# Attention values divided once per tile, loads issued in parts, row sums on ScalarE for both output matrices, six banks for turned weights, and new instruction lists

## Chip, cores and metric

The kernel runs on one core of one Trainium2 chip. The metric is the device time of one execution in microseconds; three runs were timed, and their median counts. One further execution was recorded by the profiler.

## What is computed

The input is x of shape 2 x 4096 x 512 in f32. Two residual blocks follow each other, each behind a layer norm over the 512 channels. Cut to what matters:

```python
# block 1 (RWKV mixing): xn = layernorm(x)
k = xn @ Wk.T ; r = xn @ Wr.T ; v = r
y = wkv_scan(-exp(time_decay), time_first, k, v)   # recurrence over the 4096 positions of each batch
x = x + (sigmoid(r) * y) @ Wo.T
# block 2: xn = layernorm(x); h = rmsnorm(xn, gamma1)
q = h @ Wq + bq ; kv = (h @ Wdown + bdown) @ Wup + bup      # 16 heads of 32, latent 64
att = softmax(q[t, h] . k[t, g] / sqrt(32), over g)         # heads of ONE position attend to each other
xb = xn + (att @ v) @ Wo + bo
h2 = rmsnorm(xb, gamma2) ; gate = softmax(h2 @ Wg + bg)     # 8 experts, all of them computed
x = x + xb + sum_e gate[e] * (h2 @ We[e])
```

Products of f32 numbers are made from f16 pairs: every operand is split into a high and a low half, and three matmuls (high-high, low-high, high-low) stand for one.

## The kernel before

**Tiles.** The 8192 positions are cut into 32 tiles of 256 positions, with the two batches in turn. A tile passes through three stages: mixing (steps `pre_*`, `mix_*`), attention over heads (`att_*`) and the closing stage (`fin_*`, `moe_gate`, `moe`). The last holds 16 units `moe 0` to `moe 15` (8 experts by 2 halves of the tile), each 12 matmuls into one of two PSUM banks, from which VectorE adds the gated result to `acc` (L1311). Unit u + 2 on TensorE waits until unit u has been added.

**Order.** Each engine works through a list written out in the file: `PE_HEAD`, `PE_ORDER`, `PE_TAIL`, and the same for `DVE` (VectorE), `ACT` (ScalarE), `POOL` (GpSimd) and `SP` (SyncE, which issues the DMAs). An entry is (step, part, tile). `pipeline` runs the head once, the order 27 times (once for each tile in the middle) and the tail once. Several tiles are in work at a time: an iteration of the loop finishes units of one tile while it runs the attention of the next and the mixing of the one after. Waits stand inside the steps. A step that waits holds back all that stands behind it in its engine's list.

**Set-up.** The head of each list also prepares the weights. `set_load` and `set_experts` on SyncE load all of them; the weights lie in homes borrowed from tiles that are used later. `set_max` on VectorE takes the largest absolute value of every row block, `set_bound` on GpSimd the largest over the partitions, `set_scale` on VectorE the scales made from it. For the experts the bound is a row sum of absolute values instead, made on ScalarE (`set_abs`, L782). The matrices `k`, `r` and `o1` are turned by TensorE (`set_turn`, L1346) into `turned(n)`, which is one of two PSUM banks in turn; ScalarE writes the high half (`set_hi`, L772) and VectorE the low half (`set_lo`, L1090). The experts are scaled in place (`set_times`, L788), split by ScalarE (L770), and their low half is made on GpSimd (L686).

**Attention's end.** For k = 0 to 7, `att_probs k` on TensorE makes 4 groups of 66 columns in one bank: 32 values' high parts and the sum of the probabilities, then 32 low parts and a column of zeros. `att_probs k` on VectorE divides by the sum: a reciprocal of 4 columns (L1250), a reduction that adds high and low part (L1251) and a product (L1253). `fin_back` then transposes `on` in 32 x 32 blocks (L1261), ScalarE writes the high half (L911), VectorE the low half, and `fin_project` on TensorE uses them. The bank of `att_probs k` on TensorE is free for `k + 2` when L1251 has read it.

In ScalarE's head list, all 16 steps `set_abs` of the experts stand ahead of `mix_turn` of tile 0:

```python
    ("set_decay", 0, -1), ("pre_norm", 0, 0), ("set_k", 0, -1), ("set_k", 1, -1), ("set_r", 0, -1),
    ("set_abs", 0, -1), ("set_abs", 1, -1), ("set_abs", 2, -1), ("set_r", 1, -1), ("set_abs", 3, -1),
    ...
    ("set_abs", 13, -1), ("set_o1", 1, -1), ("set_abs", 14, -1), ("set_abs", 15, -1), ("mix_turn", 0, 0),
```

Of the kernel before, what the change touches and what calls it, by code (L numbers as in the profile page):

```python
# [122 lines left out]
def att_before(use):  # L123
# [45 lines left out]
    ("att_scores", 7, 4), ("att_probs", 6, 4), ("moe", 8, 5), ("att_probs", 7, 4), ("mix_turn", 0, 2), ("moe", 9, 5),  # L169
    ("mix_k", 0, 2), ("mix_v", 0, 2), ("att_turn", 0, 3), ("fin_project", 0, 4), ("att_latent", 0, 3),  # L170
    ("att_q", 0, 3), ("moe", 10, 5), ("att_up", 0, 3), ("moe", 11, 5), ("moe", 12, 5), ("moe", 13, 5), ("moe", 14, 5),
    ("moe", 15, 5), ("att_max", 0, 3), ("fin_turn2", 0, 4), ("att_max", 1, 3), ("fin_gate", 0, 4), ("moe", 0, 4),
    ("moe", 1, 4), ("att_max", 2, 3), ("att_max", 3, 3), ("moe", 2, 4), ("att_m", 0, 3), ("moe", 3, 4), ("moe", 4, 4),
    ("att_scores", 0, 3), ("att_scores", 1, 3), ("moe", 5, 4), ("att_probs", 0, 3), ("att_scores", 2, 3),
    ("moe", 6, 4), ("att_probs", 1, 3), ("att_scores", 3, 3), ("att_probs", 2, 3), ("att_scores", 4, 3),
    ("moe", 7, 4), ("att_probs", 3, 3), ("att_scores", 5, 3), ("moe", 8, 4), ("att_probs", 4, 3),
    ("att_scores", 6, 3), ("att_probs", 5, 3), ("att_scores", 7, 3), ("mix_project", 0, 2), ("att_probs", 6, 3),
    ("att_probs", 7, 3), ("mix_turn", 0, 1), ("moe", 9, 4), ("mix_k", 0, 1), ("mix_v", 0, 1), ("att_turn", 0, 2),
    ("moe", 10, 4), ("moe", 11, 4), ("att_latent", 0, 2), ("att_q", 0, 2), ("moe", 12, 4), ("att_up", 0, 2),
    ("moe", 13, 4), ("moe", 14, 4), ("fin_project", 0, 3), ("moe", 15, 4), ("att_max", 0, 2), ("att_max", 1, 2),  # L180
    ("fin_turn2", 0, 3), ("att_max", 2, 2), ("att_max", 3, 2), ("att_m", 0, 2), ("att_scores", 0, 2),
    ("att_scores", 1, 2), ("moe", 0, 3), ("att_probs", 0, 2), ("att_scores", 2, 2), ("att_probs", 1, 2),
    ("att_scores", 3, 2), ("fin_gate", 0, 3), ("moe", 1, 3), ("att_probs", 2, 2), ("att_scores", 4, 2),
    ("att_probs", 3, 2), ("att_scores", 5, 2), ("mix_project", 0, 1), ("att_probs", 4, 2), ("att_scores", 6, 2),
    ("moe", 2, 3), ("att_probs", 5, 2), ("att_scores", 7, 2), ("att_probs", 6, 2), ("moe", 3, 3), ("moe", 4, 3),
    ("att_probs", 7, 2), ("moe", 5, 3), ("moe", 6, 3), ("moe", 7, 3), ("moe", 8, 3), ("att_turn", 0, 1),
# [1405 lines left out]
```

## Time and profile before

| | |
|---|---|
| median of 3 runs | 2910.02 us (2909.48 to 2913.99) |
| the profiled execution | 2906.95 us, its span 2905.1 us |
| TensorE (PE) busy, share of the span | 2618.6 us, 90% |
| VectorE (DVE) | 2453.4 us, 84% |
| ScalarE (ACT) | 1522.6 us, 52% |
| GpSimd (POOL) | 1006.4 us, 35% |
| mean granted TensorE clock | 0.978 |
| chain that ended last, by engine | PE 54%, DVE 32%, ACT 6% |

The span runs from the first to the last instruction. Busy time counts the work that an engine did, not its waits. In rows with an "idle before" the arrow names what ended the wait. A timeline row that says x24 stands for 24 instructions merged.

### The profile page before, as it was taken

To read this page: it belongs to the slowest core of one execution; us is meant where nothing else is said; L and a number is where in the kernel's file an instruction comes from. 1 tells how busy PE (TensorE), PEld (TensorE's weight loads), DVE (VectorE), ACT (ScalarE), POOL (GpSimd) and SP (SyncE) were. 2 spreads that over 40 slices of the span, in tenths; PEclk is the share of its full clock that TensorE was granted. 3 is DMA by queue.
4 is the path that set the end of the run, shared out by engine and by line. 5 is a ranking of instruction groups with operands and counts; after the bars stand their busy time and mean duration, and the time that the engine had idled before them with its cause. 6 is when DMAs were issued, how large, how long until landed. Compare 5 with 4: busy or idle time off the path is not lost.

```text
span 2905.1 us, 49052 instructions
## 1 busy us (share of the span) xinstructions
PE 2618.6 (90%) x18896; PEld 1579.7 (54%) x18896; DVE 2453.4 (84%) x4353; ACT 1522.6 (52%) x2783; POOL 1006.4 (35%) x970
## 2 busy tenths in 40 slices
PE   2447999999999999999999999999999999999899
PEld 2324555555556555555655555555555555565454
DVE  5688888889888888988888898888889888888853
ACT  5664555555555555555555555555555555554531
POOL 0354333334333333433333343333333333333320
PEclk9768999999999999999999999999999999999999
DMA  6011111111111101111110111111011111111110
GB/s 213 15 30 30 38 37 16 29 32 37 38 37 32 21 26 35 37 38 38 23 30 23 38 37 37 37 23 28 26 37 38 38 38 22 26 28 37 30 23 15
DMA packets 579083, 102.51 MB, mean 35 GB/s; under 512 B 547346, under 2 KB 547474, under 8 KB 578834
## 3 DMA queue, kind: packets, MB, share of 16 engines
q1 hardware_dynamic: 578852, 99.39, 16.5%
q8 instruction: 150, 2.46, 0.4%
q14 instruction: 81, 0.66, 0.1%
HBM read 48.49 MB, written 16.78 MB: 22 GB/s over the span
## 4 chain that ended last, share of the span: by engine, by line
PE 54%; DVE 32%; ACT 6%; issue 4%; POOL 2%; SPq 1%; DMA 0%; DVEq 0%; ACTq 0%; POOLq 0%
PE bank L1333 49%; DVE wkv L1134 4%; DVE ks L1219 3%; PE bank L1355 3%; DVE acc L1311 3%; DVE zz L1158 2%; DVE wkv L1123 2%; DVE e L1147 2%; DVE ev L1167 2%; DVE on L1253 2%; DVE zz L1130 2%; DVE mcol L1234 1%; DVE h2t L1096 1%; ACT ot L923 1%; DVE hrow L1225 1%
## 5 line engine op out<-in xcount | busy, mean ns | idle before, releaser
L1333 PE MATMUL bank<-w_e,h2t 128*128 128x512 f16 x6144 | 1392.8, 380 | 72.9 <-DVE acc L1311 52.6
L1333 PEld LDWEIGHTS bank<-w_e,h2t 128*128 128x128 f16 x6144 | 587.3, 98 | 754.6 <-DVE acc L1311 77.1
L1311 DVE SCALAR_TENSOR_TENSOR acc<-bank,gates,acc 128x512 f32<-128x512 f32 x512 | 376.6, 741 | 136.6 <-PE bank L1333 132.3
L727 POOL TENSOR_TENSOR pr<-pr 128x512 f16<-128x512 f32 x256 | 307.1, 1200 | 281.9 <-ACT pr L901 279.2
L899 ACT ACTIVATE pr<-bank,plog,col 128x512 f32<-128x512 f32 x256 | 197.1, 770 | 201.0 <-PE bank L1501 201.0
L1134 DVE TENSOR_TENSOR_SCAN wkv<-e,wkv 128x256 f32<-128x256 f32 x256 | 255.9, 1040 | 22.9 <-ACT e L827 19.6
L696 POOL TENSOR_TENSOR zz<-wkv,zz 128x512 f32<-128x512 f32 x64 | 106.7, 1667 | 432.2 <-DVE ev L1145 432.2
L1333 PE MATMUL bank<-w_o,xo 128*128 128x512 f16 x768 | 176.1, 387 | 49.7 <-DVE xo L1096 49.5
L1158 DVE RECIPROCAL zz<-zz 128x256 f32<-128x256 f32 x128 | 218.5, 1729 | 0.0
L901 ACT ACTIVATE pr<-bank,plog,col 128x512 f16<-128x512 f32 x256 | 197.0, 770 | 0.0
L1333 PE MATMUL bank<-xo,w_k 128*128 128x256 f16 x1536 | 175.6, 275 | 12.0 <-DVE xo L1096 12.0
L1234 DVE TENSOR_REDUCE mcol<-bank 128x4 f32<-128x512 f32 x256 | 160.7, 681 | 19.0 <-PE bank L1488 19.0
L1333 PE MATMUL bank<-w_o,oo 128*128 128x512 f16 x768 | 172.6, 382 | 0.9 <-DVE oo L1096 0.9
L1333 PE MATMUL bank<-xo,w_r 128*128 128x256 f16 x1536 | 172.9, 273 | 0.0
L1333 PE MATMUL bank<-ht,w_q 128*128 128x256 f16 x1536 | 172.9, 273 | 0.0
L1333 PEld LDWEIGHTS bank<-xo,w_k 128*128 128x128 f16 x1536 | 149.2, 99 | 31.6 <-DVE xo L1096 12.9
L1333 PEld LDWEIGHTS bank<-ht,w_q 128*128 128x128 f16 x1536 | 150.3, 98 | 17.4
L1333 PEld LDWEIGHTS bank<-xo,w_r 128*128 128x128 f16 x1536 | 150.2, 98 | 17.4
L1333 PEld LDWEIGHTS bank<-w_o,xo 128*128 128x128 f16 x768 | 73.7, 99 | 141.9 <-DVE xo L1096 55.2
L709 POOL TENSOR_TENSOR x<-x,bo_row 128x512 f32<-128x512 f32 x64 | 92.5, 1466 | 161.8 <-ACT x L854 161.8
L743 POOL TENSOR_TENSOR acc<-x,x 128x512 f32<-128x512 f32 x64 | 80.3, 1276 | 173.1 <-DMA result<-acc 173.1
L714 POOL TENSOR_TENSOR qo<-t,qo 128x256 f16<-128x256 f32 x128 | 109.4, 862 | 84.6 <-ACT qo L884 84.6
(197 smaller groups left out, 4297.7 us busy)
## 6 DMA issues: line engine op xcount, KB each, us to landing
qs<-qo SPq DMA_DIRECT2D x384, 64.0 KB, 2.4
xk<-in_attn_x SPq DMA_DIRECT2D x32, 512.0 KB, 4.8
x<-in_attn_x SPq DMA_DIRECT2D x32, 512.0 KB, 3.9
result<-acc SPq DMA_DIRECT2D x32, 512.0 KB, 2.8
ks<-k SPq DMA_DIRECT2D x128, 64.0 KB, 2.4
w_e<-in_ffn_We SPq DMA_DIRECT2D x7, 1024.0 KB, 14.2
qs<-in_attn_Wk SPq DMA_DIRECT2D x1, 1024.0 KB, 5.8
ks<-in_attn_Wr SPq DMA_DIRECT2D x1, 1024.0 KB, 8.0
```

The lines of the kernel that those rows point to most:

```text
L696: nc.gpsimd.tensor_tensor(zz[:, :, :], wkv[:, 2, :, 0:T], zz[:, :, :], ALU.add).then_inc(mix_pool.sem, 1)
L709: nc.gpsimd.tensor_tensor(x2[:, s, :], x2[:, s, :], bo_row[:, :], ALU.add).then_inc(att_pool.sem, 1)
L714: nc.gpsimd.tensor_tensor(grouped(dst, 1)[:, :, b, :], t32[:, b % 2, :].rearrange("p (g j) -> p g j", g=G), grouped(dst, 0)[:, :, b, :], A ...
L727: nc.gpsimd.tensor_tensor(pr16[:, 1, k % 2, :], pr[:, k % 2, :], pr16[:, 0, k % 2, :], ALU.subtract).then_inc(att_pool.sem, 1)
L899: nc.scalar.activation(pr[:, k % 2, :], att_bank[ATT_BANK["S", k]][:, :], ACT.Exp, bias=plog[:, 0:1], scale=colof["soft"])\
L901: nc.scalar.activation(pr16[:, 0, k % 2, :], att_bank[ATT_BANK["S", k]][:, :], ACT.Exp, bias=plog[:, 0:1], scale=colof["soft"])\
L1134: V.tensor_tensor_scan(wkv[:, n, c, 1:T + 1], e1[:, c, :], src[:, c, :], wkv[:, n, c, 0:1], ALU.mult, ALU.add).then_inc(mix_dve.sem, 1)
L1158: V.reciprocal(zz[:, c, :], zz[:, c, :]).then_inc(mix_dve.sem, 1)
L1219: V.tensor_copy(ks[n * HD:(n + 1) * HD, :, f, :], grouped(k16, 0)[f * HD:(f + 1) * HD].rearrange("p g b j -> p g (b j)")).then_inc(att_dve ...
L1234: V.tensor_reduce(mcol[:, 4 * k:4 * k + 4], att_bank[ATT_BANK["M", k]][:, :].rearrange("p (g x) -> p g x", g=4), AX, ALU.max).then_inc(att ...
L1311: V.scalar_tensor_tensor(out=acc[:, s, :], in0=moe_bank[u % 2][:, :], scalar=gates[:, s, e:e + 1], in1=acc[:, s, :], op0=ALU.mult, op1=ALU ...
L1333: ins = nc.tensor.matmul(dst, left(a), right(b), start=(n == 0), stop=(n == last))
```

## The change

1. `att_probs` on VectorE keeps only the reduction, which now covers 33 columns (32 values and the sum) and writes into `on`, widened from 32 to 33 columns a group. `fin_back` begins with one reciprocal of 32 sums and one product over the whole 128 x 1024 tile, each waited for, before the transpose.
2. `set_load` is cut into five parts and `set_experts` into eight, in the same order as before. The residual rows of tile 0 (`mix_k 0`) are now loaded ahead of the masks.
3. `o1` and `o2` are bounded by ScalarE's row sums too (8 more blocks in `set_abs`, `SUMMED`), no longer by `set_max` on VectorE.
4. `turned(n)` goes through six PSUM banks.
5. All lists are new. In ScalarE's head `mix_turn` of tile 0 now stands third, and `set_abs` is spread between the steps of tile 0; `mix_k` and `mix_v` of tile 0 stand ahead of `set_o1` on TensorE; the scaling and splitting of the experts stands later.

```diff
-MAXED = ["k", "r", "o1", "q", "o2", "small", "experts"]
+MAXED = ["k", "r", "q", "small", "experts"]
+SUMMED = ["o1", "o2"] + [f"e{e}" for e in range(E)]
+TURN_BANKS = [0, 1, 4, 5, 6, 7]
...
-        on = sb("on", [P, G, HD])
+        on = sb("on", [P, G, HD + 1])
...
-            return bank[n % 2][:, :]
+            return bank[TURN_BANKS[n % len(TURN_BANKS)]][:, :]
...
-                name = f"e{k // 2}"
+                name = SUMMED[k // 2]
...
             def att_probs(t, k):
                 pv = att_bank[ATT_BANK["PV", k]][:, 0:4 * VW].rearrange("p (g d) -> p g d", g=4)
-                og = on[:, 4 * k:4 * k + 4, :]
...
-                V.reciprocal(rden[:, 4 * k:4 * k + 4], pv[:, :, HD]).then_inc(att_dve.sem, 1)
-                V.tensor_reduce(og, pv.rearrange("p g (l d) -> p g d l", l=2)[:, :, 0:HD, :], AX, ALU.add).then_inc(att_dve.sem, 1)
-                dve.wait_ge(*att_dve.done(t, "norm", 3 * k + 1))
-                V.tensor_tensor(og, og, rden[:, 4 * k:4 * k + 4].unsqueeze(2).to_broadcast([P, 4, HD]), ALU.mult).then_inc(att_dve.sem, 1)
+                V.tensor_reduce(on[:, 4 * k:4 * k + 4, :], pv.rearrange("p g (l d) -> p g d l", l=2), AX, ALU.add).then_inc(att_dve.sem, 1)
...
-                    dve.wait_ge(summed, E * CB)
-                V.transpose(ot32.rearrange("p b (g j) -> p g b j", g=G), on[:, :, :].rearrange("p g (b j) -> p g b j", b=CB)).then_inc(fin_dve.sem, 1)
+                    dve.wait_ge(summed, len(SUMMED) * CB)
+                V.reciprocal(rden[:, :], on[:, :, HD]).then_inc(fin_dve.sem, 1)
+                dve.wait_ge(*fin_dve.done(t, "den"))
+                V.tensor_tensor(on[:, :, 0:HD], on[:, :, 0:HD], rden[:, :].unsqueeze(2).to_broadcast([P, G, HD]), ALU.mult).then_inc(fin_dve.sem, 1)
+                dve.wait_ge(*fin_dve.done(t, "quot"))
+                V.transpose(ot32.rearrange("p b (g j) -> p g b j", g=G), on[:, :, 0:HD].rearrange("p g (b j) -> p g b j", b=CB)).then_inc(fin_dve.sem, 1)
...
-                    if n >= 2:
-                        pe.wait_ge(lo_done, n - 1)
+                    if n >= len(TURN_BANKS):
+                        pe.wait_ge(lo_done, n - len(TURN_BANKS) + 1)
```

The loop's lists, cut to where the order differs (both begin at another point of the same circle):

```diff
 PE_ORDER, from unit 2 on
-    ("moe", 2, 3), ("moe", 3, 3), ("att_scores", 0, 2), ("att_scores", 1, 2), ("moe", 4, 3), ("moe", 5, 3), ("att_probs", 0, 2),
-    ("att_scores", 2, 2), ("att_probs", 1, 2), ("att_scores", 3, 2), ("moe", 6, 3), ("att_probs", 2, 2),
-    ("att_scores", 4, 2), ("moe", 7, 3), ("att_probs", 3, 2), ("att_scores", 5, 2), ("att_probs", 4, 2),
-    ("att_scores", 6, 2), ("mix_project", 0, 1), ("att_probs", 5, 2),
-    ("att_scores", 7, 3), ("mix_turn", 0, 1), ("moe", 8, 4), ("att_probs", 6, 3), ("att_probs", 7, 3), ("mix_k", 0, 1),
+    ("moe", 2, 3), ("moe", 3, 3), ("att_scores", 0, 2), ("moe", 4, 3), ("att_scores", 1, 2), ("moe", 5, 3), ("att_probs", 0, 2),
+    ("att_scores", 2, 2), ("att_probs", 1, 2), ("att_scores", 3, 2), ("moe", 6, 3), ("att_probs", 2, 2),
+    ("att_scores", 4, 2), ("att_probs", 3, 2), ("att_scores", 5, 2), ("moe", 7, 3), ("att_probs", 4, 2),
+    ("att_scores", 6, 3), ("att_probs", 5, 3), ("att_scores", 7, 3), ("mix_project", 0, 2), ("att_probs", 6, 3),
+    ("att_probs", 7, 3), ("mix_turn", 0, 1), ("moe", 8, 4), ("mix_k", 0, 1),
 DVE_ORDER, from unit 0 on
-    ("moe", 0, 3), ("moe", 1, 3), ("att_m", 0, 2), ("mix_sum", 1, 1), ("moe", 2, 3), ("mix_value", 1, 2), ("mix_scan", 1, 2),
-    ("moe", 3, 4), ("mix_rec", 2, 2), ("moe", 4, 4), ("moe", 5, 4), ("att_probs", 0, 3), ("att_probs", 1, 3),
-    ("mix_rec", 3, 2), ("mix_gate", 1, 2), ("att_probs", 2, 3), ("mix_split", 1, 2), ("pre_stats", 0, 1),
+    ("moe", 0, 4), ("moe", 1, 4), ("att_m", 0, 3), ("mix_sum", 1, 2), ("mix_value", 1, 2), ("moe", 2, 4), ("moe", 3, 4),
+    ("mix_scan", 1, 2), ("mix_rec", 2, 2), ("moe", 4, 4), ("moe", 5, 4), ("mix_rec", 3, 2), ("att_probs", 0, 3),
+    ("att_probs", 1, 3), ("mix_gate", 1, 2), ("att_probs", 2, 3), ("att_probs", 3, 3), ("mix_split", 1, 2),
...
-    ("moe", 8, 4), ("att_probs", 6, 3), ("att_probs", 7, 3), ("att_stats", 0, 2), ("att_norm", 0, 2), ("fin_back", 0, 3),
-    ("mix_decay", 0, 1), ("att_turn", 0, 2), ("moe", 9, 4), ("mix_sum", 0, 1), ("mix_value", 0, 1),
+    ("att_probs", 6, 3), ("att_probs", 7, 3), ("att_stats", 0, 2), ("att_norm", 0, 2), ("fin_back", 0, 3),
+    ("mix_decay", 0, 1), ("moe", 8, 4), ("att_turn", 0, 2), ("moe", 9, 4), ("mix_sum", 0, 1), ("mix_value", 0, 1),
```

In GpSimd's loop `mix_sum 1` now stands ahead of `att_rest` instead of behind it, and in ScalarE's loop `mix_num 1` stands behind `att_scores 3` instead of behind `att_scores 0`.

## Rows read from the trace of the kernel before

**Rows 1.** Busy time per engine in stretches; x counts instructions.

```profile
core 0: us, PE busy (x) PEld busy (x) DVE busy (x) ACT busy (x) POOL busy (x), PEclk, DMA share, GB/s
0.00:62.00 62.00, 13.35 (x56) 11.12 (x56) 30.77 (x97) 31.16 (x82) 2.07 (x11) 1.00 0.77 250
...
126.00:253.00 127.00, 67.59 (x531) 49.60 (x529) 101.33 (x150) 84.11 (x156) 67.51 (x64) 0.74 0.17 26
...
400.00:2600.00 2200.00, 2090.84 (x15247) 1260.30 (x15246) 1948.55 (x3423) 1171.19 (x2120) 789.03 (x753) 1.00 0.16 32
2592.00:2906.00 314.00, 290.62 (x1949) 163.49 (x1947) 205.10 (x379) 124.79 (x227) 82.82 (x83) 0.97 0.13 24
...
1486.59:1571.65 85.06, 80.80 (x596) 48.79 (x593) 75.46 (x133) 45.22 (x82) 30.29 (x29) 1.00 0.17 32
```

**Rows 2.** TensorE's waits, 400 to 2600 us: total us, times, longest.

```profile
PE bank L1333 <- DVE acc L1311: 50.1, 51, 2.0
PE bank L1512 <- DVE on L1251: 19.8, 24, 0.8
PE bank L1333 <- DVE h2t L1096: 19.5, 26, 1.0
PE bank L1333 <- DVE xo L1096: 12.5, 24, 0.5
```

**Rows 3.** Groups of VectorE's instructions over the whole span.

```profile
L1311 DVE SCALAR_TENSOR_TENSOR acc<-bank,gates,acc 128x512 f32<-128x512 f32 x512 | 376.6, 741 | 136.6 <-PE bank L1333 132.3 <-issue 0.7
L1134 DVE TENSOR_TENSOR_SCAN wkv<-e,wkv 128x256 f32<-128x256 f32 x256 | 255.9, 1040 | 22.9 <-ACT e L827 19.6
L1158 DVE RECIPROCAL zz<-zz 128x256 f32<-128x256 f32 x128 | 218.5, 1729 | 0.0
...
L1253 DVE TENSOR_TENSOR on<-on,rden 128x128 f32<-128x128 f32 x256 | 130.5, 510 | 8.8
...
L1251 DVE TENSOR_REDUCE on<-bank 128x128 f32<-128x256 f32 x256 | 100.3, 392 | 0.0
...
L1250 DVE RECIPROCAL rden<-bank 128x4 f32<-128x4 f32 x256 | 43.4, 170 | 12.2 <-PE bank L1513 12.2
...
L1229 DVE TENSOR_TENSOR vp<-hrow,vp 128x1024 f16<-128x1024 f32 x32 | 39.0, 1219 | 1.1 <-ACT vp L906 1.1
```

**Rows 4.** Instructions on tile `on`: shortest, median, longest in ns.

```profile
L1253 DVE TENSOR_TENSOR on<-on,rden x256: 291/292/1296, 185.4 to 2842.2; 128x128 f32<-128x128 f32 x128
```

**Rows 5.** Timeline of TensorE, where tile 3's and tile 17's `mix_k` begin.

```profile
295.60 2.67 PE L1333 MATMUL bank<-xo,w_k 128*128 128x256 f16 x23
...
1486.59 5.40 PE L1333 MATMUL bank<-xo,w_k 128*128 128x256 f16 x48
```

**Rows 6.** Timeline of TensorE, the two largest waits of one iteration.

```profile
1464.98 2.76 PE L1333 MATMUL bank<-w_e,h2t 128*128 128x512 f16 x12 [1.60 <-DVE acc L1311]
...
1475.54 0.20 PE L1512 MATMUL bank<-vp,pr 128*128 128x66 f16 x1 [0.83 <-DVE on L1251]
```

**Rows 7.** Timeline of VectorE in that iteration.

```profile
1459.13 1.75 DVE L1147 TENSOR_TENSOR e<-e,v 128x512 f32<-128x512 f32 x1
...
1494.67 1.29 DVE L1096 SCALAR_TENSOR_TENSOR oo<-ot,oo 128x512 f16<-128x512 f32 x2 [1.79 <-ACT oo L911]
```

**Rows 8.** Timeline of ScalarE at the start.

```profile
37.39 0.63 ACT L782 ACTIVATE ot<-w_e 128x512 f32<-128x512 f32 x1 [10.63 <-DMA w_e<-in_ffn_We]
...
60.50 0.63 ACT L782 ACTIVATE ot<-acc 128x512 f32<-128x512 f32 x1
...
79.00 0.69 ACT L813 ACTIVATE v<-bank,col 128x512 f32<-128x512 f32 x1 [1.93 <-PE bank L1333]
...
82.94 6.22 ACT L788 ACTIVATE w_e<-w_e,scl 128x512 f32<-128x512 f32 x10
```

**Rows 9.** Timeline of TensorE at the start.

```profile
66.68 7.04 PE L1333 MATMUL bank<-xo,w_k 128*128 128x256 f16 x48 [10.43 <-DVE xo L1096]
...
112.50 7.98 PE L1333 MATMUL bank<-w_o,xo 128*128 128x512 f16 x24 [33.53 <-DVE xo L1096]
```

More of the change, by code:

```diff
@@ L166 @@
+    ("att_scores", 5, 2), ("moe", 7, 3), ("att_probs", 4, 2),
 ]
 PE_TAIL = [
[L169 to L186, printed above, removed]
-    ("moe", 9, 3), ("moe", 10, 3), ("moe", 11, 3), ("att_latent", 0, 1), ("att_q", 0, 1), ("moe", 12, 3),
@@ L217 @@
-    ("pre_norm", 0, 2), ("set_g", 0, -1), ("mix_project", 0, 1), ("mix_turn", 0, 2), ("att_probs", 2, 0),
-    ("att_probs", 3, 0), ("att_probs", 4, 0), ("att_probs", 5, 0), ("mix_decay", 0, 2), ("att_probs", 6, 0),
-    ("att_probs", 7, 0), ("att_stats", 0, 1), ("att_norm", 0, 1), ("fin_back", 0, 0), ("mix_sum", 0, 2),
-    ("att_turn", 0, 1), ("mix_value", 0, 2), ("mix_scan", 0, 2), ("fin_project", 0, 0), ("att_latent", 0, 1),
-    ("mix_rec", 0, 2), ("mix_rec", 1, 2), ("mix_gate", 0, 2), ("mix_split", 0, 2), ("mix_decay", 1, 2),
@@ L222 @@
[L222 to L224 removed]
+    ("mix_turn", 0, 0), ("set_scale", 0, -1), ("set_max", 2, -1), ("set_k", 0, -1), ("set_k", 1, -1),
+    ("set_r", 0, -1), ("set_r", 1, -1), ("set_max", 3, -1), ("mix_decay", 0, 0), ("set_scale", 1, -1),
+    ("mix_sum", 0, 0), ("mix_value", 0, 0), ("mix_scan", 0, 0), ("mix_rec", 0, 0), ("mix_rec", 1, 0),
@@ new lines @@
+    ("mix_gate", 0, 0), ("set_o1", 0, -1), ("mix_split", 0, 0), ("mix_decay", 1, 0), ("set_o1", 1, -1),
+    ("mix_sum", 1, 0), ("mix_value", 1, 0), ("mix_scan", 1, 0), ("mix_rec", 2, 0), ("mix_rec", 3, 0),
+    ("mix_gate", 1, 0), ("mix_split", 1, 0), ("pre_stats", 0, 1), ("pre_norm", 0, 1), ("set_max", 4, -1),
+    ("set_q", 0, -1), ("set_q", 1, -1), ("mix_project", 0, 0), ("mix_turn", 0, 1), ("set_d", 0, -1),
+    ("att_stats", 0, 0), ("set_scale", 2, -1), ("att_norm", 0, 0), ("mix_decay", 0, 1), ("set_u", 0, -1),
@@ new lines @@
+    ("pre_stats", 0, 2), ("mix_split", 1, 1), ("att_probs", 0, 0), ("att_probs", 1, 0), ("pre_norm", 0, 2),
+    ("mix_project", 0, 1), ("mix_turn", 0, 2), ("set_g", 0, -1), ("att_probs", 2, 0), ("att_probs", 3, 0),
+    ("mix_decay", 0, 2), ("att_probs", 4, 0), ("att_probs", 5, 0), ("att_probs", 6, 0), ("att_probs", 7, 0),
+    ("att_stats", 0, 1), ("att_norm", 0, 1), ("mix_sum", 0, 2), ("mix_value", 0, 2), ("mix_scan", 0, 2),
+    ("att_turn", 0, 1), ("mix_rec", 0, 2), ("att_latent", 0, 1), ("fin_back", 0, 0), ("mix_rec", 1, 2),
@@ L243 @@
-    ("mix_gate", 1, 3), ("att_probs", 0, 4), ("moe", 5, 5), ("mix_split", 1, 3), ("att_probs", 1, 4),
-    ("att_probs", 2, 4), ("moe", 6, 5), ("pre_stats", 0, 2), ("att_probs", 3, 4), ("att_probs", 4, 4),
-    ("pre_norm", 0, 2), ("moe", 7, 5), ("att_probs", 5, 4), ("mix_project", 0, 3), ("att_probs", 6, 4),
-    ("att_probs", 7, 4), ("mix_turn", 0, 2), ("fin_back", 0, 4), ("att_stats", 0, 3), ("att_norm", 0, 3),
-    ("moe", 8, 5), ("mix_decay", 0, 2), ("att_turn", 0, 3), ("mix_sum", 0, 2), ("mix_value", 0, 2),
@@ new lines @@
+    ("att_probs", 4, 4), ("moe", 6, 5), ("mix_project", 0, 3), ("att_probs", 5, 4), ("mix_turn", 0, 2),
+    ("att_probs", 6, 4), ("moe", 7, 5), ("att_probs", 7, 4), ("att_stats", 0, 3), ("fin_back", 0, 4),
+    ("att_norm", 0, 3), ("moe", 8, 5), ("mix_decay", 0, 2), ("att_turn", 0, 3), ("mix_sum", 0, 2),
+    ("mix_value", 0, 2), ("fin_project", 0, 4), ("mix_scan", 0, 2), ("moe", 9, 5), ("mix_rec", 0, 2),
+    ("att_latent", 0, 3), ("mix_rec", 1, 2), ("mix_gate", 0, 2), ("moe", 10, 5), ("moe", 11, 5), ("mix_split", 0, 2),
@@ new lines @@
+    ("att_probs", 2, 3), ("att_probs", 3, 3), ("mix_split", 1, 2), ("pre_stats", 0, 1), ("att_probs", 4, 3),
+    ("pre_norm", 0, 1), ("moe", 6, 4), ("moe", 7, 4), ("mix_project", 0, 2), ("mix_turn", 0, 1), ("att_probs", 5, 3),
+    ("att_probs", 6, 3), ("att_probs", 7, 3), ("att_stats", 0, 2), ("moe", 8, 4), ("att_norm", 0, 2),
+    ("mix_decay", 0, 1), ("fin_back", 0, 3), ("att_turn", 0, 2), ("moe", 9, 4), ("moe", 10, 4), ("mix_sum", 0, 1),
+    ("mix_value", 0, 1), ("fin_project", 0, 3), ("mix_scan", 0, 1), ("mix_rec", 0, 1), ("mix_rec", 1, 1),
@@ L388 @@
+    ("att_m", 0, 1), ("moe_store", 0, 2), ("moe_store", 0, 1),
 ]
```

403 lines of the change are left out of this document (207 added, 196 removed), and 3 rows, old and new, of the table POOL_HEAD.

## The prediction

> **What bounds the kernel now.** I read first the busy time by stretches, then TensorE's waits, then the timelines of one iteration and of the start.
>
> In the middle of the run TensorE is busy 2090.84 of 2200 us at full granted clock, VectorE 1948.55, and nothing else is near [rows 1]. So the loop is bound by TensorE, and its idle time is what a better VectorE or a better order can give. From tile 3's `mix_k` to tile 17's, 14 iterations take 1486.59 - 295.60 = 1190.99 us, 85.07 each [rows 5]; in one of them TensorE works 80.80 us and stands 4.26 [rows 1]. Nearly all of that is VectorE being late: per iteration (26 of them in the window) 1.93 us for an eviction of an expert unit, 0.76 for the reduction behind `att_probs`, 0.75 for `h2t`, 0.48 for `xo` [rows 2]. It is the same in every iteration: the two largest waits stand in the timeline as 1.60 and 0.83 us [rows 6]. The most that 27 iterations can give is 27 x 4.26 = 115 us.
>
> The head is another kernel. Over the first 62 us ScalarE is busy 31.16 us and TensorE 13.35 [rows 1]: ScalarE waits 10.63 us for the first expert's weights, sums until 60.50 + 0.63 us, and only then turns to tile 0 [rows 8]; TensorE starts `mix_k` at 66.68 and `mix_project` at 112.50, after 33.53 us for VectorE [rows 9]. The steady order begins with tile 3 at 295.60 [rows 5].
>
> **The change part by part.**
>
> *One division per tile.* Eight times a tile VectorE loses a reciprocal of 170 ns and a product of 510 ns [rows 3]. The product alone takes 291 ns (shortest and median); the mean is 510 because the slowest take 1296 [rows 4]. These stood beside a GpSimd instruction on f32 tiles, as did the 1.75 us instruction at 1459.13 [rows 7]. Removed: 8 x (0.170 + 0.510) = 5.4 us busy. Added: eight columns more in each reduction, under 0.1 us in all by 392 ns for 256; a reciprocal of 32 columns, between 0.17 us (4) and 1.73 us (256) [rows 3], taken by a straight line as 0.36; a product of 1024 elements, bounded by 1.22 us for 1024 elements with two SBUF sources below [rows 3] and by eight times 0.51 = 4.1 above; I take 1.22, because a single instruction meets GpSimd once and in that iteration GpSimd has no work there. Net 5.4 - 0.1 - 0.36 - 1.22 = 3.7 us of 75.46 on VectorE.
>
> Where it lies: the 1.6 us added stand in `fin_back`, ahead of the low half `oo`, which waits 1.79 us for ScalarE today [rows 7]. ScalarE is late there because it evicts `mix_k` and normalises first, so the added work is covered; without that cover it would push back `mix_decay`, `moe 8` and `att_turn` by 1.6. The rows of 33 columns are read by the transpose with another stride; no row shows that, I take nothing, and if it cost the transpose half again (0.6 us) VectorE's saving would still be 3.1.
>
> What the saving and the new order are worth I work out by walking one iteration through both lists, with a unit of 12 matmuls at 2.6 us start to start, an eviction at 0.74, a scan at 1.04 [rows 3] and the other steps at their lengths in that iteration's timeline. In the profile, units 2 and 3 end at 1460.2, but `mix_value` (one instruction held to 1.75 us [rows 7] by GpSimd's `att_rest`) and `mix_scan` keep VectorE from evicting unit 3 until 1464.9, and unit 5 starts at 1464.98 [rows 6]. In the new lists `att_rest` stands behind `mix_sum`, `mix_value` ends at about 1458.7, units 2 and 3 are evicted by 1461.2, and TensorE runs units 4 and 5 without a wait, to 1466.3 instead of 1467.6. VectorE then has `mix_scan`, `mix_rec 2`, units 4 and 5 and `mix_rec 3` until 1469.0. `att_probs 0` to `2` on TensorE are not held; `att_probs 3`, which now follows `att_scores 4` at once, waits about 0.7 us for GpSimd's low half (1470.9). `mix_split` on VectorE ends at about 1474.5, `mix_project` starts at 1475.0 instead of 1476.67, the next `mix_k` at 1484.9 instead of 1486.59 [rows 5]. From there to unit 2 the neighbours are the old ones, with their 0.75 for `h2t`. So 1.7 us, of which the waits give 1.60 + 0.83 + 0.48 = 2.9 and the new one takes 0.7, the rest being small new delays. The second half of the walk gives some tenths more; I take 1.8 us an iteration. Bounds: 0 (each wait removed comes back elsewhere, VectorE still being 84% busy) and 3.2 (three quarters of the 4.26 go). 27 x 1.8 = 49 us, with 0 to 86.
>
> *What is moved past.* The eviction of unit 8 stood ahead of `att_probs 6` and now stands behind `fin_back` and `mix_decay`. TensorE's unit 10 waits for it. By the walk it ends 1.2 us before TensorE asks.
>
> The Trainium skill, GPSIMD Engine Reference, Key points, says that GpSimd shares its SBUF interfaces with VectorE and contends with VectorE instructions that have two SBUF inputs. The spread from 291 to 1296 ns agrees [rows 4]. By that rule the new long product could be held for one GpSimd instruction, about 1 us by that spread, and the saving would be 2.7 instead of 3.7 us.
>
> *The head.* ScalarE's `mix_turn` no longer waits for the experts' sums. TensorE's `mix_k` of tile 0 then needs only the low half of `k`: the six banks and the order put that at about 23 us instead of 66.68. But ScalarE still has the sums of the first expert ahead of its eviction of `k`, and the weights arrive at 37.39 as before, since the loads keep their order. So that eviction comes at about 39, that of `v` at 42 instead of 79.00 [rows 8]: 37 us earlier. From there to `mix_project` it took 112.50 - 79.00 = 33.5 us. In the new lists `set_scale 1` and `set_o1` (by their instructions' count and lengths in the timeline an estimated 4.5 and 2.8 us) and on ScalarE 14 steps of two sums stand between, and the experts' low halves on GpSimd, which slowed the last products by 1.6 us, are gone. Walked through, `mix_scan` of the first half begins at about 48, its `mix_split` ends at 61, the second half at 79: `mix_project` about 33 us earlier. Loads cut into parts cost nothing: same DMAs, same order. The 4.6 us of `set_max` for `o1` and `o2` go, but VectorE waited for the constants there anyway.
>
> Then some is given back. Behind that point the new lists have on ScalarE all 32 blocks of `set_times` (0.61 us each by 6.22 for ten [rows 8]) and the splits, of which some 18 us were done earlier, and on VectorE an estimated 8 us of `set_d`, `set_u`, `set_o2` and `set_scale 2`, less the 3.7 us of the division. From 126 to 253 us VectorE was busy 101.33 of 127 and ScalarE 84.11 [rows 1]; both have room for this, but not without friction. I take 3 us lost: head 30 us. Bounds: 38 (nothing given back, and the shorter divisions used) and 12 (the 18 us of ScalarE all on the path, and 3 more).
>
> *The tail.* 314 us with 290.62 of TensorE [rows 1]; two more tiles pass attention and closing stage there. 2 x 1.8, so 4 us, with 0 to 8.
>
> **Sum.** Against the profiled execution of 2906.95 us: -30 - 49 - 4 = 2824. The median is 3.07 above that execution, so 2827 us.
>
> **The rivals.**
>
> *The loop gives nothing (B).* TensorE's waits move to other places. For it: VectorE is 89% busy in the loop, and the order around `h2t` is unchanged. Against it: the two largest waits have a named cause that the new order removes. 2910 - 30 - 3 = 2877.
>
> *The loop closes nearly up (C).* The 0.7 us at `att_probs 3` does not come, and what VectorE saves pulls all evictions forward. 2910 - 30 - 86 - 3 = 2791.
>
> *The head's gain is given back (E).* Tile 0's `fin_turn2` waits on ScalarE for all experts' low halves. GpSimd starts them some 14 us of work later in its list. If that ends last, and the loop gives nothing, the time stays within 6 us of 2910. Against it: GpSimd was busy 67.51 of 127 us there [rows 1].
>
> *Slower (D): unit 8's eviction.* If `fin_back` is not covered (1.6 us), is held by GpSimd (1.0) and then misses ScalarE again (1.8), the eviction comes 4.4 us later, 3.2 us past the margin of 1.2, in each iteration. Then 27 x (3.2 - 1.8) = 38 us are lost, the head's 30 gained: 2918. It decides from 4.1 us of delay on. Against it: the eviction of `mix_k` by ScalarE, not `fin_back`, sets the time of `oo` today. That the lengthened product is the start of this delay is what the rule of the GPSIMD page would give.
>
> **How the numbers follow.** A 0.60, B 0.17, C 0.15, E 0.03, D 0.05. The predicted time is A's, 2827, its own range 2795 to 2862 (loop 1 to 2.9 us an iteration, head 20 to 35). The range for 8 in 10 takes in B and most of C: 2783 to 2882. A change of 0.2% is about what a measurement of this kernel can tell from none. Faster by more than that: A, B, C, 0.92. Within it: E, 0.03. Slower: D, 0.05.
>
> **What would show it.** In the profile after: TensorE's `mix_k` of tile 0 starts near 23 us and `mix_project` near 79; the iteration is 83.3 us, with no wait over 1 us for an eviction of units 4 or 5; L1251's group is alone in `att_probs` at about 0.40 us, and one product of about 1.2 us a tile stands in `fin_back`; tile 3's `mix_k` starts near 266 us. The prediction is wrong if `att_probs` or unit 10 on TensorE collects a new wait of over 2 us, if the long product takes 3 us or more, or if tile 0's `fin_turn2` waits for the experts' low halves.

## The result, and the profile after

The changed kernel takes 2795.18 us (2793.62 to 2796.41, 4 runs) against 2910.86 us before on the same chip: a ratio of 0.9601, 95% interval 0.9584 to 0.9617. It is 4% faster. That is 32 us less than predicted, inside the range, and at the value of rival C (2791) rather than of the case I had held likeliest, at the very edge of whose own range (2795 to 2862) it lies.

Busy time per engine in stretches after, to be read against [rows 1]; the fourth line is the last 313 us, most of the tail:

```profile
core 0: us, PE busy (x) PEld busy (x) DVE busy (x) ACT busy (x) POOL busy (x), PEclk, DMA share, GB/s
0.00:62.00 62.00, 22.84 (x152) 19.17 (x152) 34.52 (x99) 29.87 (x71) 4.79 (x13) 0.80 0.82 257
126.00:253.00 127.00, 78.63 (x581) 50.80 (x582) 102.19 (x155) 95.65 (x171) 80.87 (x73) 0.75 0.17 32
400.00:2500.00 2100.00, 2057.07 (x15115) 1254.51 (x15114) 1797.16 (x3021) 1165.31 (x2096) 727.88 (x742) 1.00 0.17 33
...
2480.00:2794.00 314.00, 293.74 (x1933) 163.02 (x1930) 197.72 (x332) 124.07 (x226) 81.55 (x83) 0.97 0.13 25
```

In the middle of the run TensorE is now busy 98% of the time (95% before) and VectorE 86% (89%). In the one iteration whose two windows stand further down VectorE works 44.64 + 25.63 = 70.3 us, where 75.46 stood [rows 1]: 5.2 us less. TensorE's waits in that stretch, total us, times, longest:

```profile
PE bank L1343 <- DVE h2t L1106: 18.5, 25, 0.7
PE bank L1522 <- POOL pr L736: 15.6, 27, 0.7
PE bank L1343 <- DVE acc L1321: 8.8, 25, 0.6
```

Of the four waits of [rows 2], the one for `on` and the one for `xo` have left the list, the one for `acc` is down from 50.1 to 8.8 us, `h2t` is as it was, and one has come: for GpSimd's low half of `pr`. Together they are 42.9 us in 25.6 iterations, 1.7 us an iteration; before, TensorE stood 4.26 us in one.

TensorE's timeline: start and length of `mix_k` and `mix_v` of tile 0 and of `mix_project` of tile 0, of tile 3's `mix_k`, and in the middle of the run one iteration's start, its wait for `h2t`, and its end:

```profile
24.41 6.40 PE L1343 MATMUL bank<-xo,w_k 128*128 128x256 f16 x48
42.96 7.34 PE L1343 MATMUL bank<-xo,w_r 128*128 128x256 f16 x48 [12.15 <-ACT xk L816]
85.61 8.17 PE L1343 MATMUL bank<-w_o,xo 128*128 128x512 f16 x24 [33.56 <-DVE xo L1106]
...
263.86 5.40 PE L1343 MATMUL bank<-xo,w_k 128*128 128x256 f16 x48
...
1411.12 5.40 PE L1343 MATMUL bank<-xo,w_k 128*128 128x256 f16 x48
...
1457.20 2.76 PE L1343 MATMUL bank<-w_e,h2t 128*128 128x512 f16 x12 [0.74 <-DVE h2t L1106]
...
1493.05 5.40 PE L1343 MATMUL bank<-xo,w_k 128*128 128x256 f16 x48
```

These starts give the account used for every run below: how early the steady order begins (tile 3's `mix_k`), what an iteration takes (tile 3's `mix_k` to tile 30's, divided by 27), and the tail (from there to the end of the span). Head, loop and tail of the changed kernel: 263.86, 81.95 and 316.5 us; of the kernel before 295.60, 85.04 and 313.5 us. The gain of 112.1 us in the span is so 31.7 from the head, 83.4 from the loop (27 x 3.09), and -3.0 from the tail. The prediction had 30, 49 and 4. (The medians are 115.7 us apart, since the profiled execution of the kernel before was 3.9 us faster than its median.)

The division, by the instructions on tile `on` (shortest, median, longest in ns) that answer to [rows 3, 4]:

```profile
L1259 DVE TENSOR_REDUCE on<-bank x256: 369/423/433, 154.2 to 2725.6; 128x132 f32<-128x264 f32 x128
L1267 DVE RECIPROCAL rden<-on x32: 344/348/353, 194.7 to 2728.8; 128x32 f32<-128x32 f32 x32
L1269 DVE TENSOR_TENSOR on<-on,rden x32: 1224/1225/1682, 195.1 to 2729.1; 128x1024 f32<-128x1024 f32 x32
L1271 DVE STREAM_TRANSPOSE ot<-on x32: 1245/1245/1246, 196.8 to 2730.4; 128x1024 f32<-128x1024 f32 x32
```

### The profile page after: what moved, and what is told of

Same layout as the page of the kernel before. It is cut to its first block, busy times and chain, and to the rows that moved or that the text cites. A ratio compares the mean times of both kernels' runs of the same rounds, so it can differ in the third digit from the quotient of the medians.

```text
span 2793.0 us, 48627 instructions
## 1 busy us (share of the span) xinstructions
PE 2605.8 (93%) x18896; PEld 1583.4 (57%) x18896; DVE 2292.0 (82%) x3903; ACT 1532.3 (55%) x2799; POOL 950.7 (34%) x970
## 4 chain that ended last, share of the span: by engine, by line
PE 81%; DVE 8%; ACT 5%; POOL 2%; issue 2%; SPq 1%; DVEq 0%; ACTq 0%; POOLq 0%
PE bank L1343 72%; PE bank L1365 3%; DVE mcol L1244 2%; PE bank L1481 2%; PE bank L1511 2%; DVE h2t L1106 1%; ACT pr L910 1%; POOL pr L736 1%; PE bank L1522 1%; DVE acc L1321 1%; ACT pr L908 1%; POOL w_e L695 1%; PE bank L1498 1%; ACT h2t L941 1%; DVE ks L1229 1%
## 5 line engine op out<-in xcount | busy, mean ns | idle before, releaser
L1144 DVE TENSOR_TENSOR_SCAN wkv<-e,wkv 128x256 f32<-128x256 f32 x256 | 245.0, 997 | 17.9 <-ACT e L836 16.7
L816 ACT ACTIVATE xk<-bank,col 128x512 f32<-128x512 f32 x64 | 43.8, 687 | 195.4 <-PE bank L1343 195.4
L723 POOL TENSOR_TENSOR k<-t,k 128x256 f16<-128x256 f32 x128 | 94.4, 738 | 141.4 <-ACT k L893 138.1
```

Of the source, the lines that this page charges most:

```text
L723: nc.gpsimd.tensor_tensor(grouped(dst, 1)[:, :, b, :], t32[:, b % 2, :].rearrange("p (g j) -> p g j", g=G), grouped(dst, 0)[:, :, b, :], A ...
L1144: V.tensor_tensor_scan(wkv[:, n, c, 1:T + 1], e1[:, c, :], src[:, c, :], wkv[:, n, c, 0:1], ALU.mult, ALU.add).then_inc(mix_dve.sem, 1)
```

## The experiments

Two ideas stood against each other from here. Theory O: the time comes from the orders of work (the new lists). Theory V: it comes from the work that VectorE no longer has (one division per tile). All runs in one table; head, loop and tail as above, from one profiled execution each, and each ratio against the kernel before on the same chip:

| kernel | mix_k of tile 0 | of tile 3 | iteration | tail | median us | ratio to before (95%) |
|---|---|---|---|---|---|---|
| before | 66.68 | 295.60 | 85.04 | 313.5 | 2910.86 | |
| changed | 24.41 | 263.86 | 81.95 | 316.5 | 2795.18 | 0.9601 (0.9584 to 0.9617) |
| e1_bank_division | 23.75 | 265.67 | 84.71 | 319.5 | 2872.57 | 0.9867 (0.9852 to 0.9882) |
| e2_division_alone | 69.08 | 295.67 | 83.21 | 316.3 | 2859.89 | 0.982 (0.9805 to 0.9834) |
| e3_sums_first | 61.49 | 285.23 | 81.97 | 315.8 | 2818.56 | 0.9679 (0.9663 to 0.9695) |
| e4_two_banks | 29.50 | 269.98 | 81.97 | 316.0 | 2801.32 | 0.9621 (0.9607 to 0.9635) |
| e5_first_tile_ahead | 23.31 | 253.35 | 81.98 | 318.3 | 2788.22 | 0.9573 (0.9556 to 0.959) |
| e6_unit7_ahead | 23.60 | 263.35 | 85.16 | 319.1 | 2883.70 | 0.9903 (0.9888 to 0.9917) |
| e8_scan_ahead | 22.67 | 263.55 | 82.82 | 316.4 | 2820.03 | 0.9686 (0.9671 to 0.97) |
| e9_product_twice | 22.63 | 263.82 | 82.00 | 318.9 | 2798.49 | 0.961 (0.9596 to 0.9625) |
| e10_unit3_early | 69.27 | 295.01 | 82.62 | 315.1 | 2843.24 | 0.9773 (0.9759 to 0.9786) |
| e11_unit3_unit7 | 71.61 | 297.83 | 82.70 | 318.4 | 2843.66 | 0.9774 (0.976 to 0.9787) |
| e12_tail_unit | 22.98 | 251.29 | 81.99 | 319.9 | 2786.96 | 0.9575 (0.9562 to 0.9588) |

Two cautions for the table. Kernels with the same head differ at tile 3 by up to 2.8 us (295.01 to 297.83; 263.35 to 265.67; 253.35 and 251.29), so a difference of that size in the head is not a reading. And tile 30's `mix_k` stands in the tail's list of TensorE, which in the old lists has one expert unit more ahead of it (unit 9): 70 units are left from there on, 71 in the new lists. So with the old lists 2.6 us of work counts in the loop, 0.10 us an iteration, that with the new lists counts in the tail.

**Lists without the division, division without the lists.** e1 is the changed kernel with the old steps of `att_probs` and `fin_back`:

```diff
-                V.tensor_reduce(on[:, 4 * k:4 * k + 4, :], pv..., AX, ALU.add)
+                V.reciprocal(rden[:, 4 * k:4 * k + 4], pv[:, :, HD])
+                V.tensor_reduce(og, pv...[:, :, 0:HD, :], AX, ALU.add)
+                V.tensor_tensor(og, og, rden[...].to_broadcast([P, 4, HD]), ALU.mult)
```

> The changed kernel with its new lists, but with the division made for each bank again (reciprocal, reduction and product eight times a tile, nothing added in fin_back). Theory O (the new order gives the loop its gain): the iteration stays at 82.0 to 82.8 us and the time at 2795 to 2820. Theory V (the VectorE time set free gives it): VectorE has 4 to 5 us more in each iteration, TensorE waits for evictions again, the iteration is 84.3 us or more and the time 2860 or more.

e2 is the reverse edit in the kernel before: the division once per tile, all lists, heads and banks as they were.

> The kernel before with its old lists, and only the division moved to fin_back, once per tile. Theory O: the wait of 1.6 us for the eviction of unit 3 stays, as mix_scan still stands ahead of it; only the 0.8 at att_probs shrinks: iteration 84.2 to 85.1 us, time 2885 to 2912. Theory V: the iteration falls under 83.3 us and the time under 2860.

Both went against theory O. The iteration, old lists first: 85.04 with the old division and 83.21 with the new; in the new lists 84.71 and 81.95. So the division gives 1.83 us in the old lists and 2.76 in the new; the lists give 0.33 with the old division and 1.26 with the new. Nothing adds up singly: 1.83 + 0.33 is 2.16, and both together give 3.09. The median distance from one `mix_k` to the next between tiles 3 and 29, which leaves out the unit named above, says the same: 84.97 and 83.07 us in the old lists, 84.73 and 81.92 in the new, so 1.90 and 0.24 singly and 3.05 together. The waits say why. First e1, 400 to 2500 us; then one iteration of e2 (its wait for unit 5, as in [rows 6]):

```profile
PE bank L1522 <- DVE on L1261: 34.9, 50, 1.0
PE bank L1365 <- ACT xk L802: 27.6, 25, 1.1
PE bank L1343 <- DVE h2t L1106: 17.8, 24, 0.7
PE bank L1343 <- DVE xo L1106: 9.2, 25, 0.4
PE bank L1343 <- DVE acc L1321: 8.9, 25, 0.9
```

```profile
1522.70 2.76 PE L1333 MATMUL bank<-w_e,h2t 128*128 128x512 f16 x12 [1.60 <-DVE acc L1311]
```

In e1 the new order has removed the 1.60 us for unit 3's eviction, but with eight divisions among the same steps VectorE is late at the next places: TensorE waits twice for `on` (0.98 and 0.41 us), 0.37 us for `xo`, and then, at its `mix_turn`, 1.10 us for ScalarE's `pre_norm`, which has itself stood 4.13 us for VectorE's `nb`. In e2 the division has removed the waits for `on` and `xo`, and the 1.60 us, which is a matter of order alone, is untouched. The head belongs to the rest of the change (lists, loads, sums and banks), not to the division: tile 3's `mix_k` stands at 265.67 in e1, at 295.67 in e2.

**Which order.** e8 puts, in the changed kernel, VectorE's evictions of units 2 and 3 where they were around `mix_value` and `mix_scan`:

```diff
-("mix_value", 1, 2), ("moe", 2, 4), ("moe", 3, 4), ("mix_scan", 1, 2),
+("moe", 2, 4), ("mix_value", 1, 2), ("mix_scan", 1, 2), ("moe", 3, 4),
```

> The changed kernel with VectorE's evictions of units 2 and 3 around mix_value and mix_scan again, as in the old list. If this order is what the new list adds to the division: TensorE waits 1.5 us or more for the eviction of unit 3, iteration 83.0 to 83.6, time 2822 to 2840. Rival (with VectorE's spare time the order no longer matters): under 82.3, time under 2805.

It cost 0.87 us an iteration (82.82), somewhat less than expected. Its waits:

```profile
PE bank L1523 <- POOL pr L737: 24.9, 27, 1.0
PE bank L1344 <- DVE acc L1322: 24.6, 50, 0.6
```

Unit 5 waits only 0.63 us, not 1.60: `mix_value` is not held by GpSimd in this kernel (its second product takes 0.69 us in the mean, not 1.75), which had been the other half of that delay. Beside it the wait for `pr` is longer, 0.96 us for 0.58. e10 does the opposite from the other side: the kernel before, with the new division and one move, unit 3's eviction ahead of `mix_scan`:

```diff
-("mix_value", 1, 2), ("mix_scan", 1, 2), ("moe", 3, 4),
+("mix_value", 1, 2), ("moe", 3, 4), ("mix_scan", 1, 2),
```

> The old lists and heads, the new division, and one move in VectorE's list of the loop: unit 3's eviction stands ahead of mix_scan 1 instead of behind it. Single-move theory: what the lists bring to the loop once the division is out of it (83.21 us to 81.95 us per iteration) comes mostly from this order, since its reverse cost the changed kernel 0.87 us: iteration 82.2 to 82.5 us, median 2832 to 2840 us. Joint theory: the lists bring it only together (the removed wait for unit 3 returns at the next wait, for GpSimd's low half or for unit 7's bank): iteration 82.9 to 83.2 us, median 2851 to 2860 us. The head is the old one in both: tile 3's mix_k at 295 to 296 us.

It fell between the two (82.62): the wait of 1.60 us is gone, and 1.02 of it has come back three steps later, at `att_probs 1`, as this line of its timeline shows:

```profile
1515.71 0.19 PE L1513 MATMUL bank<-vp,pr 128*128 128x66 f16 x1 [1.02 <-POOL pr L728]
```

So one transposition of two entries holds 0.59 of the 1.26 us that the lists are worth beside the new division. TensorE, no longer held at unit 5, arrives at `att_probs 1` before GpSimd has the low half; in the changed kernel the wait for GpSimd stands at `att_probs 3` and is 0.58. What holds the other 0.67 us was not taken apart.

**Unit 7.** e6 is the changed kernel with unit 7 at its old place in TensorE's list, e11 is e10 with unit 7 at its new one:

```diff
-("att_scores", 4, 2), ("att_probs", 3, 2), ("att_scores", 5, 2), ("moe", 7, 3),
+("att_scores", 4, 2), ("moe", 7, 3), ("att_probs", 3, 2), ("att_scores", 5, 2),
```

> The changed kernel with unit 7 on TensorE ahead of att_probs 3 again, the old place. If the 0.6 us for GpSimd's low half is simply covered: iteration 81.3 to 81.5, time 2779 to 2786. Rival (att_scores 5 comes later by a unit, and ScalarE's mix_split behind it too, so mix_project waits for xo): iteration 81.9 to 82.6, time 2793 to 2815.

> As the run before, and in TensorE's list unit 7 stands behind att_scores 5 instead of behind att_scores 4. Single-move theory for unit 7: its reverse cost the changed kernel 3.2 us, so the two moves together should reach 81.9 to 82.2 us per iteration and 2824 to 2831 us. Rival: the place of unit 7 matters only where GpSimd, ScalarE and mix_project stand as in the new lists; with the old ones, in which mix_project comes ahead of att_probs 5 and gives it cover, the move gives nothing or costs up to 0.6 us (a wait for GpSimd's low half at att_probs 3 as in the changed kernel): the iteration is that of the run before, or up to 0.6 us longer.

e6 was the surprise of the study, outside both of its expectations: 3.2 us more an iteration, 88 us in all, for one unit moved by two entries to fill a wait of 0.6 us. Its largest wait, then what stands around it in one iteration, and the windows over the wait and over the `mix_project` behind it (PEclk is 1.00 in the rest of the iteration):

```profile
PE bank L1523 <- POOL pr L737: 60.1, 25, 2.4
```

```profile
1444.90 0.19 PE L1523 MATMUL bank<-vp,pr 128*128 128x66 f16 x1 [2.41 <-POOL pr L737]
...
1445.36 7.04 PE L1344 MATMUL bank<-w_o,xo 128*128 128x512 f16 x24
```

```profile
1442.00:1445.30 3.30, 0.89 (x25) 0.75 (x22) 1.41 (x3) 3.22 (x5) 1.15 (x1) 1.00 0.00 0
1445.30:1452.40 7.10, 7.10 (x34) 2.99 (x32) 5.21 (x12) 3.14 (x5) 3.14 (x4) 0.76 0.00 0
```

The unit had been the cover of ScalarE's and GpSimd's chain for the scores 5, and without it `att_probs 5` stands 2.41 us. Then comes a second bill: `mix_project` takes 7.04 us where it takes 5.35 elsewhere, at a mean granted clock of 0.76, so part of it ran at the lower level (1.2 GHz). 2.41 us of new wait and 1.69 us of slower matmuls, less the 0.58 us of the wait that went, make 3.5, against 3.2 measured; the slower `mix_project` comes in 25 of the 27 iterations and the wait in 26, which makes it 3.3. In the 3.30 us of the first window TensorE had been busy 0.89, with matmuls of 0.19 and 0.38 us. The Trainium skill, TensorE: Matmul & The Clock Gate, What's actually happening, says that the granted clock is set by how busy TensorE has been recently; the trace agrees in that the clock fell behind this nearly idle stretch. The length of the wait does not settle it: the first such wait of e6 was as long, and `mix_project` behind it took 5.35 us at a clock of 1.00.

```profile
337.58 0.19 PE L1523 MATMUL bank<-vp,pr 128*128 128x66 f16 x1 [2.42 <-POOL pr L737]
338.04 5.35 PE L1344 MATMUL bank<-w_o,xo 128*128 128x512 f16 x24
```

In the old lists, where another order of the neighbours stands around it, the move of unit 7 does nothing: e11 has e10's iteration, waits and median, as the rival said.

**The long product.** e9 does the product in `fin_back` twice, which adds 1.2 us ahead of `oo`:

```diff
+                V.tensor_tensor(ot..., on[:, :, 0:HD], rden[...].to_broadcast([P, G, HD]), ALU.mult)
                 V.tensor_tensor(on[:, :, 0:HD], on[:, :, 0:HD], rden[...].to_broadcast([P, G, HD]), ALU.mult)
```

> The changed kernel with a second product of 1.22 us in fin_back, whose result is overwritten. If fin_back is covered by the 2.55 us that oo waits for ScalarE: no change, 2792 to 2799. Rival (it pushes back mix_decay, unit 8 and att_turn, each iteration by 1.2): 2815 or more.

The iteration is 82.00 instead of 81.95 us, the median 2798.49 us, both as expected if it is covered: the cover behind which I put the product is there, and has room for a second. In the changed kernel VectorE's timeline shows it, 2.55 us of waiting for ScalarE behind the product and the transpose:

```profile
1414.16 1.23 DVE L1269 TENSOR_TENSOR on<-on,rden 128x1024 f32<-128x1024 f32 x1
...
1419.21 1.29 DVE L1106 SCALAR_TENSOR_TENSOR oo<-ot,oo 128x512 f16<-128x512 f32 x2 [2.55 <-ACT oo L920]
```

**The head.** e3 lets ScalarE bound all the experts' weights before tile 0 again (all 20 entries of `set_abs` stand ahead of `mix_turn`, four for `o1` and `o2` among them, and VectorE's half of `mix_turn` comes later). e4 takes four of the six banks away; with two, ScalarE's `mix_num` must also stand ahead of `set_o1 1`, since else ScalarE, TensorE and VectorE wait for each other in a ring:

```diff
-TURN_BANKS = [0, 1, 4, 5, 6, 7]
+TURN_BANKS = [0, 1]
```

> The changed kernel with all row sums on ScalarE ahead of mix_turn of tile 0 again, as before, and VectorE's mix_turn of tile 0 moved behind set_max 3 so that nothing deadlocks. Theory O (tile 0 waited for the sums): mix_project of tile 0 at about 105 to 115 us, tile 3's mix_k 20 to 30 us later than 263.9, time 2815 to 2828. Rival (the head's gain is the work taken off VectorE and the six banks): under 8 us later, time under 2804.

> The changed kernel with two banks for turned weights instead of six, and ScalarE's mix_num 0 of tile 0 ahead of the second half of set_o1, without which the order would deadlock. If the banks save no time themselves: mix_k of tile 0 up to 5 us later, but ScalarE evicts k only at 42 us anyway, so the time stays within 2791 to 2799. Rival (the banks carry part of the head's gain): 2800 or more.

e3, as its theory O had it: tile 3's `mix_k` 21.4 us later, the loop untouched. e4, as its rival had it: `mix_k` of tile 0 5.1 us later, tile 3's 6.1, 6 us in the median. So of the 31.7 us some 21 are the sums' new place and some 6 the banks (with the one entry moved beside them), if the two simply add; the remainder was not taken apart.

e5 mends the new order where the profile after showed it waiting. `mix_k` was done at 31, but TensorE's `mix_v` stood 12.15 us for ScalarE's eviction of `k`, which stood behind the first expert's sums. ScalarE stands 10.43 us ahead of them, as its timeline in the changed kernel shows (the row names no releaser; in [rows 8] it is the transfer of these weights):

```profile
40.91 0.63 ACT L791 ACTIVATE ot<-w_e 128x512 f32<-128x512 f32 x1 [10.43 <-issue]
...
42.15 1.24 ACT L816 ACTIVATE xk<-bank,col 128x512 f32<-128x512 f32 x2
...
50.34 0.69 ACT L822 ACTIVATE v<-bank,col 128x512 f32<-128x512 f32 x1 [1.93 <-PE bank L1343]
```

```diff
-("set_abs", 3, -1), ("set_abs", 4, -1), ("mix_k", 0, 0), ("set_abs", 5, -1), ("mix_v", 0, 0), ("mix_exp", 0, 0),
+("set_abs", 3, -1), ("mix_k", 0, 0), ("mix_v", 0, 0), ("mix_exp", 0, 0), ("set_abs", 4, -1), ("set_abs", 5, -1),
```

with `mix_decay 0` ahead of `set_max 3` in VectorE's head.

> The changed kernel, with ScalarE's evictions of k and v of tile 0 and its first exponentials ahead of the sums of the first expert (which must wait for that expert's weights until 40.9 us), and VectorE's mix_decay 0 ahead of the wait for the constants. If that wait is what ends last in the head: v evicted at about 39 us instead of 50.3, mix_project of tile 0 at 74 to 80 instead of 85.6, tile 3's mix_k 5 to 11 us earlier than 263.9, time 2784 to 2790. Rival (GpSimd's low halves of the experts, 10% of the chain of waits from 60 to 264 us, end last): under 2 us earlier, 2793 to 2797.

TensorE's timeline of e5: `mix_v` follows `mix_k` at once, and `mix_project` starts 10.5 us earlier.

```profile
23.31 6.25 PE L1345 MATMUL bank<-xo,w_k 128*128 128x256 f16 x48
29.70 5.40 PE L1345 MATMUL bank<-xo,w_r 128*128 128x256 f16 x48
75.08 7.62 PE L1345 MATMUL bank<-w_o,xo 128*128 128x512 f16 x24 [38.23 <-DVE xo L1108]
```

All of it arrives at tile 3 (253.35 for 263.86). The median is 2788.22 us, 7 below the changed kernel: 0.2% faster than the kernel under study, 4.3% than the one before. The tail was 1.8 us longer in this run.

**The tail.** e12 is e5 with the last `att_m` one unit later, to fill TensorE's wait of 4.0 us in the tail for VectorE's maximum:

```diff
-("att_max", 3, 1), ("att_m", 0, 1), ("fin_gate", 0, 2), ("moe", 0, 2),
+("att_max", 3, 1), ("fin_gate", 0, 2), ("moe", 0, 2), ("att_m", 0, 1),
```

> The changed kernel with the first tile's set-up ahead of the experts' first sums (as in e5_first_tile_ahead, 2788.22 us) and, in TensorE's list of the tail, att_m of tile 31 one unit later, behind the unit 0 that used to follow it. In the changed kernel TensorE stands 4.0 us at that place for VectorE's last maximum, and the unit is 2.6 us of work. Cover theory: 1.3 to 2.6 us of the wait is filled, the tail falls from 318.3 us to 315.7 to 317.0 us, and the median to 2784 to 2787 us. Rival: the unit's bank or the gates behind it are the next wait, VectorE's att_m comes as much later, and the scores of the last tile start when they did: the tail stays at 318 to 318.6 us, the median at 2788 to 2789 us.

The rival has it: TensorE's longest waits in e12 from 2600 us to the end are now these, where in e5 the waits for `mcol` at `att_m` were 5.4 us and none stood for `m`, and the tail is no shorter (319.9 us).

```profile
PE bank L1349 <- DVE h2t L1112: 5.0, 3, 2.2
PE bank L1517 <- DMA qs<-m: 2.8, 1, 2.8
PE bank L1510 <- DVE mcol L1250: 1.4, 1, 1.4
```

A wait covered at `att_m` is met again as the wait for the transfer of `m`, which can only start behind it. The median of 2786.96 us can't be told from e5's; tile 3 began 2 us earlier in this run, though its head is e5's.

## Why the prediction was right, and where its sizes were off

**The bound.** Right: TensorE sets the loop, and the gain is TensorE's idle time.

**The division, as work.** Right within a tenth: 0.423 us a reduction (0.40 predicted), 0.348 for the reciprocal (0.36; the straight line gives 0.34), 1.225 for the product (1.22), and the transpose over rows of 33 costs nothing more (1.245). The rule that GpSimd could hold the product by about 1 us was weighed at nothing; of 32 products one, tile 0's, took 1682 ns and all others at most 1227, so in the loop it costs nothing. The cover in `fin_back` stands (e9), and rival D with it falls.

**What the loop gives: the term mis-sized.** I had "1.8 us an iteration"; it is 3.09, or 3.05 without the unit that the account puts elsewhere. That is above the 1 to 2.9 us of my likeliest case; the range for 8 in 10 held the result because it took in rival C. Of C's two conditions only one came: what VectorE saves did pull the evictions forward, but the wait at `att_probs 3`, which was not to come, is there. Two windows of the changed kernel show where, `mix_k` to unit 2 and unit 2 to the next `mix_k`:

```profile
1411.12:1464.06 52.94, 51.86 (x379) 33.93 (x377) 44.64 (x80) 27.40 (x56) 12.67 (x15) 1.00 0.26 50
1464.06:1493.05 28.99, 28.41 (x212) 14.96 (x213) 25.63 (x40) 18.09 (x28) 15.58 (x14) 1.00 0.01 4
```

Before, unit 2 started at 1454.98, so the second window took 1486.59 - 1454.98 = 31.6 us; it fell by 2.6, where my walk had 1.7. It hit `mix_project` nearly: 1475.0 - 1454.98 = 20.0 us after unit 2 by the walk, 1483.77 - 1464.06 = 19.7 in the profile. The new wait at `att_probs 3` was 0.7 by the walk and is 0.58. But from `mix_project` to `mix_k` I took the old distance, 9.9 us, and it is 9.28: `att_probs 5` and `att_scores 7` now stand ahead of `mix_project`, and I had counted these two behind it again. What I called "small new delays", 0.5 us off 2.9 - 0.7, stood for nothing in the lists: most of it was this miscount. The first window gives 0.4 where "some tenths more" became 0.1: the wait of 0.2 us for ScalarE's `ot` is gone, and the removed waits give back more than their idle rows (80.7 to 80.27 us busy with the same matmuls; the window of 80.80 in [rows 1] reaches 0.1 us into the next iteration).

**What VectorE is spared** was "3.7 us" and is 5.2. The division's part is as worked out (3.8 us by the means over the loop); on top of it `mix_value` is no longer held by GpSimd (1.75 to 0.68 us), and a scan takes 997 ns in the mean instead of 1040 [rows 3], eight of them an iteration 0.3 us. What is left is a balance of instructions that moved both ways: `ev<-e,ev` fell by 1.1 us an iteration, `ev<-ev,zz` rose by 0.7.

**Where it comes from.** My text gave the order ("the two largest waits have a named cause that the new order removes") most of the credit and the division none of its own. The runs say: the division alone 1.83, the order alone 0.33 (0.10 of it the unit that is counted elsewhere), both 3.09. The named cause was right for one wait (1.60) and wrong in that this wait, taken away with VectorE nearly as full as before, returns as 1.39 for `on` and 1.10 at `mix_turn` (e1). That is rival B, and it is what the lists would have met without the division.

**The head.** The sum was right (31.7 for 30) by luck, through two errors that cancel. `mix_k` at 24.41 (23 predicted). Wrong was "that of `v` at 42": I had ScalarE's eviction of `k` behind the first sums, but not that TensorE's `mix_v` needs the banks it frees; and those sums began at 40.91, not 37.39. SyncE issued the first expert's load at 33.70 us, against 30.22 before, though the order of the loads is the same (why its issues came later is open), so "the weights arrive at 37.39 as before" failed too. `v` was evicted at 50.34 and `mix_project` came at 85.61, not 79. Against that, nothing was given back: I took 3 us for the work moved behind `mix_project`, and the lead over the kernel before grew from 26.9 us there to 31.7 at tile 3. Rival E falls with it, though its sign was there in small. At tile 0's `fin_turn2` TensorE stood 9.96 us for ScalarE before and stands 1.96 now; ScalarE then does wait for the experts' low halves, 1.35 us, while TensorE works on `att_max` and is not held. First the kernel before, then the changed one:

```profile
246.59 1.97 PE L1355 MATMUL bank<-ident,ot 128*128 128x128 f32 x8 [9.96 <-ACT ot L923]
```

```profile
223.33 1.97 PE L1365 MATMUL bank<-ident,ot 128*128 128x128 f32 x8 [1.96 <-ACT ot L932]
224.62 1.31 ACT L941 ACTIVATE h2t<-bank 128x512 f16<-128x512 f32 x2 [1.35 <-POOL w_e L695]
```

**The tail.** By the account 3.0 us longer, not 4 shorter. 2.6 us of that is the unit that the new tail list has behind tile 30's `mix_k` and the old one ahead of it; TensorE's busy time in the last 314 us is 3.1 us more than before [rows 1], this unit among it. From tile 29's `mix_k` to the end it is 398.4 us in both kernels. So the tail gave nothing of the 4 us, and the runs themselves spread from 315.1 to 319.9.
